# Transposing the context by DMA instead of TensorE, from an fp16 split made by GpSimd a step early

## The reference, cut to what matters

```
x = x + tanh(g_xattn[0]) * attention(layernorm(x), ctx)     # 16 heads of 64, a null key, K and V from ctx
x = x + tanh(g_ffn[0])   * ffn(layernorm(x))                # relu, fp8 rounding of hidden and w2
x = x + tanh(g_xattn[1]) * second(layernorm(x), ctx, mask)  # rmsnorm, scan over decays of ctx[..., :256]
x = x + tanh(g_ffn[1])   * experts(layernorm(x))            # router picks 2 of 8 experts per token
```

## Time and profile before

| | |
|---|---|
| median of three runs | 1779.32 us (1778.08 to 1781.38) |
| the profiled execution | 1782.04 us, its span 1780.2 us |
| TensorE busy | 1522.6 us, 86% of the span |
| VectorE busy | 1202.0 us, 68% |
| ScalarE busy | 925.8 us, 52% |
| GpSimd busy | 592.0 us, 33% |
| mean granted TensorE clock | 0.963 of full speed |

### The profile page before, as it was taken

One profiled execution on the slowest core, in us unless ns is written; L12 is line 12 of the kernel. 1 busy time (PEld: TensorE's weight loads), 2 busy tenths in 40 slices (PEclk: granted clock), 3 DMA queues, 4 the chain that ended last, 5 costly groups with the idle time before them and its releaser, 6 DMA issues. The chain is left out here.

```text
span 1780.2 us, 36819 instructions
## 1 busy us (share of the span) xinstructions
PE 1522.6 (86%) x12540; PEld 1084.8 (61%) x12541; DVE 1202.0 (68%) x3316; ACT 925.8 (52%) x2530; POOL 592.0 (33%) x777
## 2 busy tenths in 40 slices
PE   3899999999999999999999999986538887888784
PEld 2667676676766767667676776755425454555452
DVE  5478888788887888878888788886433433333332
ACT  4377676766767667676676766755112222222221
POOL 3002323233332333323333233332423444444442
PEclk9899999999999999999999999998759999999997
DMA  7101202021020210202102021031016222222224
GB/s 241 60 1 61 66 7 72 7 67 65 9 72 7 66 61 12 72 7 67 56 18 72 2 71 49 8 109 63 20 58 177 45 44 44 44 44 44 44 44 121
DMA packets 78142, 97.97 MB, mean 55 GB/s; under 512 B 20576, under 2 KB 61680, under 8 KB 77936
## 3 DMA queue, kind: packets, MB, share of 16 engines
q1 hardware_dynamic: 51152, 77.01, 13.6%
q0 software_dynamic: 15872, 18.95, 6.6%
q10 hardware_dynamic: 10976, 0.13, 0.3%
HBM read 65.02 MB, written 35.23 MB: 56 GB/s over the span
## 5 line engine op out<-in xcount | busy, mean ns | idle before, releaser
L801 ACT ACTIVATE prob<-S,nm 128x256 f32<-128x256 f32 x512 | 235.5, 474 | 81.8 <-issue 41.2
L794 ACT ACTIVATE pTh<-T 128x512 f16<-128x512 f32 x256 | 139.5, 597 | 136.0 <-PE T L975 135.8
L1303 PE MATMUL S<-GL,xgh 128*128 x576 | 173.8, 384 | 10.1 <-issue 8.8
L1494 DVE TENSOR_REDUCE mx<-S 128x2 f32<-128x512 f32 x256 | 163.3, 679 | 21.2 <-PE S L1048 20.7
L645 POOL TENSOR_SCALAR ve_ln<-mv_ln 128x2 f32<-128x2 f32 x64 | 14.7, 229 | 470.6 <-DVE mv_ln L1468 469.7
L1506 DVE SCALAR_TENSOR_TENSOR pTl<-T,pTh 128x512 f16<-128x512 f32 x256 | 164.1, 682 | 6.5 <-ACT pTh L794 6.5
L716 POOL DMA_INDIRECT xg<-x_rows,trow x72 | 70.4, 978 | 230.2 <-DMA acc_rows<-ysb,yid 99.3
L810 ACT ACTIVATE prob<-prob,rden 128x256 f32<-128x256 f32 x256 | 116.5, 504 | 56.5 <-DVE p0n L1515 55.8
L975 PE MATMUL T<-ident,prob 128*128 128x128 f32 x1024 | 142.2, 283 | 1.6 <-DVE prob L1519 1.4
L953 ACT ACTIVATE aH<-T 128x512 f16<-128x512 f32 x72 | 43.0, 597 | 192.0 <-PE T L975 144.4
L970 PE MATMUL W<-cTh,Wkh 128*128 128x256 f16 x512 | 140.3, 274 | 0.0
(11 more groups left out here) (296 smaller groups left out, 4457.3 us busy)
## 6 DMA issues: line engine op xcount, KB each, us to landing
cx<-in_ctx_dram SPq DMA_DIRECT2D x16, 512.0 KB
gst<-in_L_ffn_gating_w_dram SPq DMA_DIRECT2D x16, 512.0 KB
gating_split<-gsp SPq DMA_DIRECT2D x16, 512.0 KB
GL<-gating_split SPq DMA_DIRECT2D x8, 1024.0 KB
stg<-in_L_xattn_Wkv_dram SPq DMA_DIRECT2D x8, 512.0 KB, 13.5
xl<-in_x_dram SPq DMA_DIRECT2D x16, 256.0 KB
lst<-in_L_ffn_linear_w_dram SPq DMA_DIRECT2D x16, 256.0 KB
xres<-in_x_dram SPq DMA_DIRECT2D x16, 256.0 KB
```

The source lines that it names most:

```text
L794: A(flat(pTh[:, h, :, :]), T[h][:, :], ACT.Copy).then_inc(s_pTh[h], 1)
L801: ins = A(prob[:, h, t, :], S[h][:, t * NTOK:(t + 1) * NTOK], ACT.Exp, bias=nm[:, h, t:t + 1], scale=SM, accum_out=rs[:, h, t:t + 1])
L1303: ins = M(o[:, :], (xgl if n == 2 else xgh)[r % 2][:, k, :], GLflat[:, bass.ds(w, HID)], start=(k == 0 and n == 0), stop=(k == KD - 1 and ...
L1494: ins = V.tensor_reduce(mx[:, h, :], S[h][:, :].rearrange("p (t k) -> p t k", t=TT), AX.X, ALU.max)
```

## The change

The two context units leave the list of units, TensorE, ScalarE and VectorE. POOL makes the high and low fp16 parts of the context, `cxh` and `cxl`, in the layout of `cx`, a cast and a subtraction of 128x1024 each (`ctx_split`); for batch i+2 in step i, behind the `ln4` factors and ahead of the split of the linear weights. SP then issues four transposing transfers per batch (`ctx_T`), each of 128x512 fp16 to four 128x128 blocks, in step i, when the last `v` unit of batch i+1 has been computed, and ahead of the store of `x4`. The first batch is split and transposed right after the setup. TensorE waits for all four transfers before `k_unit(0)`. The buffers `x4` and `x4T` share the homes of `xh` and `xn`; VectorE's wait for the store of `x4` moves from the `ln4` norm to the `ln2` norm in pair 2 of the next step.

```diff
@@ -43,7 +43,7 @@
 
 PRE, ATTN, POST = "pre", "attn", "post"
-UNITS = [("p0T", False, POST), ("ctxT", True, PRE), ("ctxT", True, PRE), ("wout", False, POST),
+UNITS = [("p0T", False, POST), ("wout", False, POST),
          ("xT", True, PRE), ("k", True, PRE), ("q", True, PRE), ("q", True, PRE),
          ("k", True, PRE), ("x1T", True, POST), ("q", True, PRE), ("q", True, PRE), ("s0", False, PRE),
          ("w1", False, POST), ("w1", False, POST), ("w1", False, POST), ("w1", False, POST), ("count", False, POST),
@@ -260,6 +260,7 @@
         xres = sb("xres", [P, TT, D])
         xn = sb("xn", [P, TT, D])
         xTh, xTl = sb("xTh", [P, KD, NTOK], FP16), sb("xTl", [P, KD, NTOK], FP16)
+        cxh, cxl = sb("cxh", [P, TT, CTX], FP16), sb("cxl", [P, TT, CTX], FP16)
         cTh, cTl = sb("cTh", [P, KC, NTOK], FP16), sb("cTl", [P, KC, NTOK], FP16)
         ns0 = [sb(f"ns0{i}", [P, TT, HEADS]) for i in range(2)]
         u = [sb(f"u{i}", [P, TT, D]) for i in range(2)]
@@ -293,8 +294,8 @@
         arg = sb("arg", [P, 2, NTOK])
         dec = sb("dec", [P, 2, NTOK])
         x3 = sb("x3", [P, TT, D])
-        x4 = sb("x4", [P, TT, D])
-        x4T = sb("x4T", [P, KD, NTOK])
+        x4 = xh
+        x4T = xn
         st = {n: sb("st_" + n, [P, TT, 6]) for n in ("ln1", "lno", "ln2", "ln3", "ln4")}
         mv = {n: sb("mv_" + n, [P, TT, 2]) for n in st}
         rstd = {n: sb("rstd_" + n, [P, TT]) for n in st}
@@ -369,6 +370,7 @@
         s_x = [sem("x_in0"), sem("x_in1")]
         s_c = [sem("ctx_in0"), sem("ctx_in1")]
         s_xr = sem("xres_in")
+        s_csh, s_cs, s_cT = sem("ctx_high"), sem("ctx_split"), sem("ctx_transposed")
         s_gw = sem("gating_in")
         s_lw = sem("linear_in")
         full = [sem(f"work_full{k}") for k in range(NWORK)]
@@ -515,6 +517,14 @@
             sp.wait_ge(s_init, 1)
             work = WorkBanks()
+            def ctx_T(b):
+                wait_apart(sp, s_cs, b.n + 1)
+                for src, dst in ((cxh, cTh), (cxl, cTl)):
+                    for t in range(TT):
+                        sp.dma_start_transpose(dst[:, :, t * P:(t + 1) * P], src[:, t, :]).then_inc(s_cT, 16)
+
+            ctx_T(Batch(0, 0))
+
             def expert_in(e):
                 if e:
                     sp.wait_ge(s_we, 32 * e)
@@ -524,10 +534,12 @@
                 sp.dma_start(GL[:, e, G_SIZE:].rearrange("p (c n) -> p c n", c=2),
                              lsplit_d[two].rearrange("c p n -> p c n")).then_inc(s_we, 16)
-            def rows_out(i, post, work):
+            def x3_out(post, work):
                 k, nfull, _ = work.at["win"][0]
                 wait_apart(sp, free[k], nfull)
                 sp.dma_start(pick(acc_v, post.n), x3[:, :, :]).then_inc(s_x3o, 16)
+
+            def x4_out(post):
                 wait_apart(sp, s_nrm["ln4"], post.n + 1)
                 sp.dma_start(pick(x4_v, post.n), x4[:, :, :]).then_inc(s_x4o, 16)
@@ -556,7 +568,13 @@
                     for e in range(early):
                         expert_in(e)
                 if POST in parts:
-                    rows_out(i, post, work)
+                    x3_out(post, work)
+                if PRE in parts and i.n + 2 < NB:
+                    k, nfull, _ = work.at["v"][3]
+                    wait_apart(sp, full[k], nfull)
+                    ctx_T(nxt)
+                if POST in parts:
+                    x4_out(post)
                 if ATTN in parts:
                     for k, nfull, _ in work.at["gT"]:
                         wait_apart(sp, free[k], nfull)
@@ -630,6 +648,15 @@
             own = StepCount(POOL_STEPS)
             work = WorkBanks()
+            def ctx_split(b):
+                pool.wait_ge(s_c[b.par], 16 * (b.half + 1))
+                at_least(pool, s_cT, 64 * b.n)
+                pool.tensor_copy(cxh[:, :, :], cx[b.par][:, :, :]).then_inc(s_csh, 1)
+                pool.wait_ge(s_csh, b.n + 1)
+                pool.tensor_tensor(cxl[:, :, :], cx[b.par][:, :, :], cxh[:, :, :], ALU.subtract).then_inc(s_cs, 1)
+
+            ctx_split(Batch(0, 0))
+
             def step(i, parts):
                 own.begin(i.n)
                 nxt, post = i.shift(1), i.shift(-1)
@@ -690,6 +717,8 @@
                     rstd_of("ln4", post, 1e-5).then_inc(s_rstd["ln4"], 1)
                     wait_apart(pool, s_rstd["ln4"], post.n + 1)
                     rms_of_normed("ln4", 1e-6).then_inc(s_rms, 1)
+                if PRE in parts and i.n + 2 < NB:
+                    ctx_split(i.shift(2))
                 if ATTN in parts:
                     wait_apart(pool, s_lw, 16 * (i.n + 1))
@@ -842,8 +871,6 @@
                     if j == 0:
                         if pre:
                             act.wait_ge(s_c[nxt.par], 16 * (nxt.half + 1))
-                            one("ctxT", 0, flat(cTh[:, 0:2, :]))
-                            one("ctxT", 1, flat(cTh[:, 2:4, :]))
                         if attn:
                             norm(j)
                         if pre:
@@ -1081,15 +1108,6 @@
                         ins = tr(o[0:HEADS, t * P:(t + 1) * P], p0n[post.par][:, t, :])
                     ins.then_inc(s, 1)
-                def ctxT_unit(m):
-                    pe.wait_ge(s_c[N_], 16 * (nxt.half + 1))
-                    o, s = bank("ctxT", m)
-                    for k in range(2):
-                        for t in range(TT):
-                            ins = tr(o[:, k * NTOK + t * P:k * NTOK + (t + 1) * P],
-                                     cx[N_][:, t, (2 * m + k) * P:(2 * m + k + 1) * P])
-                    ins.then_inc(s, 1)
-
                 def rows_T(name, src, ready):
                     pe.wait_ge(*ready)
@@ -1217,15 +1235,11 @@
                     if j == 0:
                         if post_:
                             p0T_unit()
-                        if pre:
-                            ctxT_unit(0)
-                            ctxT_unit(1)
                         if post_:
                             wout_unit()
                     if j == 1 and pre:
                         rows_T("xT", xn, (s_nrm["ln1"], nxt.n + 1))
-                        evicted("ctxT", 0)
-                        evicted("ctxT", 1)
+                        pe.wait_ge(s_cT, 64 * (nxt.n + 1))
                         k_unit(0)
                     if j == 2 and pre:
                         k_unit(1)
@@ -1654,6 +1668,7 @@
                         if pre:
                             low("xT", 0, flat(xTl[:, :, :]), flat(xTh[:, :, :]))
                     if j == 2 and post_:
+                        dve.wait_ge(s_x4o, 16 * (post.n + 1))
                         normed("ln2", post, xh, tiles(x1), rstd["ln2"]).then_inc(s_nrm["ln2"], 1)
                     if j == 5 and post_:
                         ffn_residual()
@@ -1666,8 +1681,6 @@
                     if j == 0:
                         if pre:
-                            low("ctxT", 0, flat(cTl[:, 0:2, :]), flat(cTh[:, 0:2, :]))
-                            low("ctxT", 1, flat(cTl[:, 2:4, :]), flat(cTh[:, 2:4, :]))
                             normed("ln1", nxt, xn, tiles(xl[nxt.par]), rstd["ln1"]).then_inc(s_nrm["ln1"], 1)
                         if post_:
                             attn_out()
@@ -1723,7 +1736,6 @@
                             attn_low(2)
                     if j == 7:
                         if post_:
-                            dve.wait_ge(s_x4o, 16 * (post.n + 1))
                             normed("ln4", post, x4, tiles(x3), rstd["ln4"]).then_inc(s_nrm["ln4"], 1)
                         if pre:
                             dve.wait_ge(s_rstd["ctx"], nxt.n + 1)
```

## The result

The changed kernel takes 1790.0 us (median of 5 runs, 1789.0 to 1793.3) against 1779.3 (5 runs, 1776.9 to 1781.6) for the one before: 1.0065 [1.0048, 1.0082] times as long. That is slower, as forecast, and 3 us less than the 1793 forecast. The profiled execution has a span of 1787.4 us and took 1790.0 in all, 8.0 more than that of before. Of the 8.0, 7.2 lie within the span. The rest is time outside it, which no row of a profile shows: 2.6 us here, 1.8 in the kernel before.

What follows compares the result with a forecast made beforehand. Each step was bound by DVE, POOL, DVE up to `xn`, then TensorE. Start 4.5, batch step 0 0.5, locks 8.7 and transfers 0 gave 13.7 on 1782.04: 1795.7, median 1793; range 1786 to 1802 (55%), 1776 to 1835 (8 in 10).

Steps and rivals of the forecast that it cites:

- The bound: Before `xT` in each step: TensorE, freed of at most 0.89 us, only waits longer for `xn`; worth nothing.
- what `wout` would wait for: At `wout` on TensorE: it still waits for ScalarE's eviction of `p0T`, so it starts some 0.45 us earlier.
- The start: First batch, before the first k matmul: split and four transfers have no step to hide in; 4.5 us late.
- The locks: DVE's router work: POOL's longer work holds DVE's two-input operations, making `slot` 0.67 us late in 13 steps, 8.7 us.
- The transfers: Four per batch before `k_unit(0)`: 5.7 us in a window of 13.2 us, so hidden, 0.
- The rival that they would be late: Before `k_unit(0)`: four transfers with a landing take 17.2 us, 4.0 past the window; 1868 us in all; 19%.
- The reading by which the blocks go one after the other: Transposing transfers: sixteen blocks in sequence take 21 us, 8 us too late per step, 110 us over 14 steps.
- The scatters' landing gates `rstd_lno`: Loads on SP shifted by 2 to 4 us could delay `rstd_lno`, but DVE comes to it later: 0.
- the prediction's signs of being right: Idle before `xT` about 1 us, `slot` 0.5 to 0.7 later, `pw` or `oh` over 0.3, k at 54 to 57, step 75.0.

Runs made afterwards that it cites:

- 7: Kernel before, with `rstd_ln1` ahead of the four table scatters on GpSimd and the wait for their landing behind `rstd_lno`: 1777.4 us, ratio 0.9961.
- 8: Changed kernel, with `rstd_ln1` ahead of the four table scatters on GpSimd and the wait for their landing behind `rstd_lno`: 1776.5 us, 0.9963 of the kernel before.
- 6: Changed kernel, with the first batch's context transposed by TensorE as before and the other fifteen by transfers: 1788.7 us, 1.0051 of the kernel before.
- 9: Changed kernel, with `rstd_ln1` ahead of the scatters, their landing wait behind `rstd_lno`, and the first batch transposed by TensorE: 1775.4 us, 0.9957 of the kernel before.
- 4: Changed kernel, with GpSimd's split kept but unused: TensorE transposes every context, no transposing transfers: 1786.2 us, 1.0017 of the kernel before.
- experiment 1: Changed kernel, with GpSimd's wait for the landing of the four table scatters moved behind `rstd_lno`: 1784.5 us, 1.0020 of the kernel before.

## Why the prediction was right, and where it was not

*The bound.* That TensorE's 0.89 us buy nothing, since `xn` sets `xT`, was right: the idle time grew to 0.99 us where "about 1" was forecast, and with the wait for `xn` taken away (7, 8) the same change is worth 0.37 us a step. Nearest to wrong was what `wout` would wait for: VectorE's `aTl`, not `p0T`, and 0.7 us of the 0.89 go there.

*The start.* 4.5 us forecast, 4.96 measured at the first k matmul and 4.65 at the first `slot`. Three errors inside nearly cancel, which was luck. The split took 3.24 us, not 3.68: the subtraction of this shape is 2.12 here and not the 2.37 of the earlier trace rows, and the cast 1.04, not 1.22. An issue took 1.3 us, not 0.9, so four took 5.2 and not 3.6. The landing took 1.3 us, not 2.1. The 0.9 us outside the span is in no term. And no experiment gave the whole start back: with the first batch by TensorE the first `slot` came 3.4 (6) and 2.3 us (9) earlier, and the median fell by 1.3 and 1.1. That the late start costs 4.65 us of the end is read from the trace, not shown by taking it away.

*The locks: the right mechanism, mis-sized.* 0.67 us a step was forecast, 8.7 us in all; 0.07 came, 0.8 us in twelve steps (from the undisturbed steps above; 4 has the same with the split alone). The term added a loss for `pw` and for `dl`, and took none back for the hold that `dl` had already borne in the earlier trace rows. Moreover GpSimd's chain ended 0.4 us earlier than the two too long durations made it. With `dl`'s 0.20 credited and the 0.23 that `pw` lost, the step's own method gives 0.03, and the rest of the 0.07 is spread over the small operations.

*The transfers.* Hidden in the full steps, as forecast: no k matmul waits for them. The rival that they would be late (56 us and more) is false; four issues and the landing take 6.5 us at the start and 7.4 in the plain step (593.21 to 599.33 for the issues), of a 13 us window. The packets were close to the 512 of that rival: 544 each. The Trainium skill, *VectorE: DVE Perf Modes*, "The three transpose paths", has 1309 ns for one 128x128 block. In the trace four such blocks go in one transfer, and the issues stand 1.31 us apart, so the sixteen blocks are usable 6.5 us after the first issue (49.47 to 56.01), not 21 us. The reading by which the blocks go one after the other at that price is refuted here.

*What failed: "The scatters' landing gates `rstd_lno`; loads shifted by 2 to 4 us could delay it, but DVE comes to it only behind `xn`, the `lno` statistics and the next maxima: 0."* The mechanism was named and costed at nothing. In the kernel before, the margin was already gone in two steps (idle 0.64 and 0.37 us, in the table above), and the prediction doesn't use them: the step at 660 us, on which the prediction was built, is one with ample margin (9.43 us behind `slot`). The transfers took 5.2 us of SP's time, 6.1 in the plain step, and the loads moved by 4.4 to 4.7 us against `slot`, onto the scatters. The start of `ve_lno`, which waits for them, moved by 2.2 us on the mean (10.4 to 12.6), and four of twelve steps crossed the margin. It cost some 6 us in the profiled pair, and 5.5 to 8 between the changed kernel and experiment 1.

So the total was right for a reason that was partly wrong, and its closeness is luck: 13.7 us forecast from 5.0 + 8.7 + 0. In the profiled pair the parts are 4.65 (start) + 0.8 (locks) + 6.1 (late scatters) = 11.6 us by the end of the twelve steps, of which the rest of the span gave back 4.4; by the medians the kernel is 10.7 us slower. The term for the locks was 8 us too large, and the one put at nothing held 6. Of the prediction's signs of being right, three came as it had them (the idle time before `xT`, `pw` at 0.41 us, the first k matmul at 56.0), one didn't (`slot` 0.07 us later, not 0.5 to 0.7), and one came by chance: a step is 75.05 us on the mean of twelve where 75.0 was forecast, but as eight steps of 74.4 and four long ones, and not as an equal delay in each.

## What to carry to other kernels

Work taken off a busy engine pays only if that engine sets the end of the stretch. Look at its waits first; if another order takes that wait away, try the two together: here the new order was worth nothing in the old kernel's steps and 0.43 us in each of the changed one's. An issue of 1.3 us on a queue engine is a delay for everything queued behind it: write down when each later transfer will now start, and what else is in flight at that moment. And a wait of unequal length from step to step must be judged by its worst steps, not by the one that was read closely.

## What the hardware showed that I had not expected

- A transposing transfer of 128x512 fp16 took SP about 1.3 us of issue (1.2 to 2.3), where the plain ones of the step shown take 0.37 to 0.98, and 544 packets each by the queue's count.
- GpSimd's wait for the landing of four small indirect scatters ended 9.4 to 12.6 us behind `slot` on the mean, depending on what else was in flight, and differed by 2 to 5 us between the steps of one profile.
- A GpSimd subtraction of 128x1024 took 2.12 to 2.14 us, and 2.37 in the setup.
- VectorE operations with two SBUF inputs that met GpSimd's subtraction ended within 0.04 us of its end; one that began 0.01 us behind its end took its plain 0.16.
- After an idle time of TensorE of 2.0 us the granted clock was 0.51 for 3.5 us in one place. After one of 2.12 us that ends at 105 to 114 us, it fell in three of eleven profiles, of the old and of the new kernel, and not in the other eight. With its end at 108.4 to 108.6 us it fell in two and stayed up in one.
- Kernels with transposing transfers ahead of their first batch step took 2.3 to 3.0 us outside the profile's span, the others 1.8 to 1.9.
